# Where an attention kernel loads its queries: during the projection stage, and by SyncE

## The chip, the cores and the metric

One core of one Trainium2 chip. The metric is the device time of one execution in microseconds: the median of several runs. Engines are named as in the profile: PE is TensorE, DVE VectorE, ACT ScalarE, POOL GpSimd, SP SyncE. SPq, ACTq and POOLq are the queues' own instructions, mostly DMA issues.

## What is computed

A transformer block with layer norm after each half, for x of 8 x 1024 x 256: 16 heads of width 16, relative position bias clipped to +-64, and a feed-forward layer whose weights are reduced to a sign times a row mean.

```python
qkv = q @ in_proj_weight.T + in_proj_bias          # 8 x 1024 x 768
qh = qh / sqrt(16)
scores = einsum('bhid,bhjd->bhij', qh, kh)          # 128 maps of 1024 x 1024
rel = clip(pos[None, :] - pos[:, None], -64, 64) + 64
bias = take_along_axis(einsum('bhid,rd->bhir', qh, rel_pe), rel)
attn = softmax(scores + bias); out = (attn @ vh) @ out_w.T + out_b
x = layernorm(x + out)
h = gelu(x @ bw1.T + b1); x = layernorm(x + h @ bw2.T + b2)    # bw = mean|w| * sign(w)
```

## The kernel before

Three stages follow one another, each in a block of its own with a barrier behind it.

**Projection stage** (lines 143 to 569). Eight batches, two buffer halves `a`. For each batch PE turns x (line 487, four banks), ACT copies the banks to `xT` (line 317), PE makes keys, values and queries from it (line 513, line 499, line 513), 12 banks in all. ACT writes the high parts of keys and queries (lines 327 and 336), DVE the low parts and the values (lines 403 and 418). SP stores them to DRAM: `k_scr`, `v_scr`, `q_scr` (lines 263 to 277). ACT waits on `s_store[a]` before it writes keys over those of two batches ago. Ahead of the batches PE turns the projection weights (line 451, jobs 0 to 3), and the table of relative positions is read (`relT`), its differences taken by DVE (lines 389 to 393) and copied by ACT (`rel_parts`, line 303). SP meanwhile writes zeros over the pads of `band_scr`, eight DMAs of 512 KB (line 241). Behind the batches the signs of the feed-forward weights are made and turned (lines 342 and 451), and DVE reduces them to their means (lines 433 and 442).

**Attention stage** (lines 574 to 1170). G = 64 steps, each two heads of one batch; `SLOTS` = 4 buffers for queries, keys and values. Before a step can start, its bands are made, three steps ahead: PE multiplies queries with the table (line 1042), ACT copies the product to `band_out` (line 914; in the profile `carried`), POOL fills its ends (line 829), SP writes it to `band_scr` (line 721), and POOL reads it back skewed, so that each row is shifted by its position (lines 792 to 805). DVE finds row maxima over scores plus band (lines 966 and 977), 24 units ahead, POOL negates them (line 812), PE turns them (line 1060) and SP puts them into two further rows of the queries (line 731), so that the scores come out with the maximum taken off. ACT takes the exponential (line 925), and PE multiplies with the values (line 1109). Each engine's order is written out by hand: steps from -3 to 63, eight pairs of units each (u = 0 to 15).

POOL issues all loads. At its start: the queries of steps 0 and 1, six memsets, the keys of step 0. SP's first work waits for five of the memsets (`s_set`), then writes two rows of ones into the keys (line 754). In the loop:

```python
                def step_of(i, step):
                    if 0 <= step and step + 3 < G:
                        if step > 0:
                            pool.wait_ge(s_sc, cnt(i, 2 * UNITS, step * 2 * UNITS))
                        load_queries(pool, i, step + 3)
                    read_chunk(i, step, 0)
```

`load_queries` issues four DMAs: for each of the two heads one of 128 KB, the high part twice over, and one of 64 KB. `s_sc` counts finished scores: queries of step + 3 go into the buffer that step - 1 read.

**Feed-forward stage** (lines 1172 to 1515): 16 iterations of projection, layer norm, two layers and layer norm.

Of the kernel before, what the change touches and what calls it, by code (L numbers as in the profile page):

```python
# [5 lines left out]
F32 = mybir.dt.float32  # L6
F32R = mybir.dt.float32r
# [24 lines left out]
def post_ln_block(nc, x, w_in, b_in, w_out, b_out, rel, w1, b1, w2, b2, out):  # L32
# [24 lines left out]
    with outer:  # L57
# [52 lines left out]
        x_rows = x.rearrange("b t e -> (b t) e")  # L110

# [27 lines left out]
        with ExitStack() as ctx:  # L139
# [12 lines left out]
            zeros = sb("zeros", [P, NT, P], F32)  # L152
# [5 lines left out]
            w_in_s = sb("w_in_s", [P, 6, E], F32)  # L158
            w_out_s = sb("w_out_s", [P, 2, E], F32)
# [8 lines left out]
            relT = sb("relT", [D, R], F32)  # L168
# [3 lines left out]
            alpha2_wide = sb("alpha2_wide", [P, 2, P], F32)  # L172
            s_win = sem("projection_weights_in")
            s_w = sem("other_weights_in")
# [17 lines left out]
            jobs = []  # L192
# [16 lines left out]
            xT = sb("xT", [P, 2, KE, HALF + T], F32)  # L209
            q_parts = sb("q_parts", [P, 2, PARTS, 2, T], F32R)  # L210
            k_parts = sb("k_parts", [P, 2, PARTS, 2, KCOLS - P], F32R)
            v_s = sb("v_s", [P, 2, NG, NT, HG, VC], F32)

# [17 lines left out]

            block = ctx.enter_context(nc.Block())

            @block.sync
            def _(sp):

                sp.dma_start(w_in_s[:], w_in.rearrange("(j p) e -> p j e", p=P)).then_inc(s_win, 16)
                sp.dma_start(relT[:], rel.rearrange("r d -> d r"), allow_slow_non_contiguous=True).then_inc(s_relT, 16)
                sp.wait_ge(s_set, 3)
                for a in range(SLOTS * HG):  # L240
                    sp.dma_start(flat(band_scr, a * NT * P * BAND_ROW,
                                      [[BAND_ROW, P], [P * BAND_ROW, NT], [1, P]]),
                                 zeros[:]).then_inc(s_zero, 16)
# [10 lines left out]
                with sp.Fori(0, B // 2) as i:  # L254
                    for a in range(2):
# [29 lines left out]
            def _(act):  # L285
# [10 lines left out]
                for n in range(0, 4, 2):  # L296
# [5 lines left out]
                act.wait_ge(s_dve, 3)  # L302
                nc.scalar.activation(rel_parts[:, 0, :], rel_d[:], ACT.Copy).then_inc(s_rel, 1)
                act.dma_start(b1_col[:], b1.rearrange("(j p) -> p j", p=P),
                              allow_slow_non_contiguous=True).then_inc(s_rows, 16)
                act.dma_start(bo_row[:], flat(b_out, 0, [[0, P], [1, E]])).then_inc(s_rows, 16)
                act.dma_start(b2_row[:], flat(b2, 0, [[0, P], [1, E]])).then_inc(s_rows, 16)
                with act.Fori(0, B // 2) as i:
                    for a in range(2):
# [12 lines left out]
                        act.wait_ge(s_store[a], i * 16 * STORES + 16 * STORES)  # L322
                        for m in range(2):
# [16 lines left out]
                act.wait_ge(s_w, 16 * 3)  # L340
# [3 lines left out]
                for n in range(4, len(jobs), 2):  # L344
                    evacuate(n)

            @block.gpsimd
            def _(pool):
# [7 lines left out]
                nc.gpsimd.memset(zeros[:], 0.0).then_inc(s_set, 1)  # L356
# [12 lines left out]
            def _(dve):  # L369
# [10 lines left out]
                for n in range(1, 4, 2):  # L380
# [12 lines left out]
                                        ALU.subtract).then_inc(s_dve, 1)  # L393
                dve.wait_ge(s_rel, 1)
# [52 lines left out]
            def _(pe):  # L447
# [14 lines left out]
                pe.wait_ge(s_eva, 2)  # L462
                pe.wait_ge(s_evd, 2)
                pe.wait_ge(s_dve, 1)
# [54 lines left out]
                pe.wait_ge(s_w, 16 * 3)  # L519
                pe.wait_ge(s_lo, 8 * B + 8)  # L520
                for n in range(4, len(jobs)):
# [13 lines left out]
        with ExitStack() as ctx:  # L535
# [26 lines left out]
            queries = sb("queries", [P, SLOTS, T], F32R)  # L562
# [28 lines left out]
            s_q = [sem(f"queries_in{a}") for a in range(SLOTS)]  # L591
# [11 lines left out]
            s_passed = sem("waits_passed")  # L603
            s_mm = sem("minus_max_split")
# [83 lines left out]
            def load_queries(eng, i, c):  # L688
# [871 lines left out]
```

## Time and profile before

| | us |
|---|---|
| median of 3 runs | 2368.68 |
| lowest, highest | 2364.39, 2369.45 |
| the profiled execution | 2367.33 |
| its span, from first to last instruction | 2365.6 |
| PE busy in it | 2227.5 |
| DVE, ACT, POOL busy | 1740.6, 1573.1, 1085.1 |

The projection stage fills the span up to 222.8 us; the first scores of step 0 come at 281 us. All rows below are of the one profiled execution, and their times are counted from the start of its span. An engine's busy time leaves out DMA issues and waits. In a timeline, rows that repeat are merged: the first number is the start, the second the length of the whole group.

### The profile page before, as it was taken

What the parts mean: (1) busy time and instruction counts of PE and PEld (TensorE: products, weight loads), DVE (VectorE), ACT (ScalarE), POOL (GpSimd) and SP (SyncE); (2) the same over time, 40 slices, a digit from 0 to 9 for tenths busy, and PEclk for the clock granted to TensorE, in tenths of its full rate; (3) what the DMA queues carried; (4) which work ended last, traced back from release to release, by engine and by line L of the source; (5) the groups of instructions that cost most, each with busy time, mean ns of one, the idle gap of its engine ahead of it and who ended that gap; (6) DMA issues with size and microseconds to landing.
All of it is one profiled execution on the core that took longest, in us unless ns stands there. A gap on an engine that the chain in (4) does not pass through costs nothing. (4 is left out here: it accounts for less than half of the span.)

```text
span 2365.6 us, 47819 instructions
## 1 busy us (share of the span) xinstructions
PE 2227.5 (94%) x14580; PEld 1262.2 (53%) x14580; DVE 1740.6 (74%) x3446; ACT 1573.1 (66%) x2193; POOL 1085.1 (46%) x1803
## 2 busy tenths in 40 slices
PE   7996799999999999999999999999999998899997
PEld 4554344544444444444444444444444443688886
DVE  3444677777777777777777777777777772688885
ACT  3443277777777777777777777777777776466776
POOL 1001444455444554455554545545455441567663
PEclk9998599999999999999999999999999999899999
DMA  9987877777777777777777777777777762334321
GB/s 327 363 315 270 220 204 210 212 202 208 211 209 213 199 212 212 207 211 202 209 212 210 211 201 209 216 208 211 200 211 214 209 189 71 101 102 111 111 65 45
DMA packets 334570, 468.55 MB, mean 198 GB/s; under 512 B 89797, under 2 KB 262550, under 8 KB 334486
## 3 DMA queue, kind: packets, MB, share of 16 engines
q0 software_dynamic: 120960, 215.78, 34.4%
q1 hardware_dynamic: 203030, 243.06, 32.3%
q10 hardware_dynamic: 10496, 8.79, 1.2%
q8 instruction: 29, 0.48, 0.1%
q14 instruction: 55, 0.45, 0.1%
HBM read 244.73 MB, written 221.25 MB: 197 GB/s over the span
## 5 line engine op out<-in xcount | busy, mean ns | idle before, releaser
L925 ACT ACTIVATE probs<-weigh_ps 128x1024 f32<-128x1024 f32 x1024 | 1048.9, 1025 | 471.0 <-PE weigh_ps L1092 467.4
L977 DVE CUSTOM_DVE_ANT_1 ring_ps<-ring_ps,band_all 128x512 f32<-128x512 f32 x1008 | 680.9, 715 | 264.3 <-PE ring_ps L1053 263.9
L1053 PE MATMUL ring_ps<-keys,queries 48*128 48x512 f32 x2048 | 827.4, 468 | 34.8 <-DVE partial_max L966 9.5
L1092 PE MATMUL weigh_ps<-queries,keys 50*128 50x512 f32 (+3 forms) x2688 | 751.2, 386 | 1.3 <-ACT probs L925 0.6
L966 DVE TENSOR_REDUCE partial_max<-ring_ps 128x2 f32<-128x1024 f32 x512 | 627.8, 1226 | 114.6 <-PE ring_ps L1053 79.7
L1053 PEld LDWEIGHTS ring_ps<-keys,queries 48*128 48x128 f32 x2048 | 371.1, 187 | 519.0 <-issue 398.0
L1109 PE MATMUL sum_ps<-probs,values 128*32 128x512 f32 x4096 | 546.7, 606 | 0.1
L829 POOL COPY carried<-carried 128x252 f32<-128x252 f32 x430 | 159.2, 395 | 560.8 <-ACT carried L914 560.8
L1077 PE MATMUL weigh_ps<-ident,band_all 128*128 128x128 f32 x2048 | 363.4, 290 | 19.1 <-ACT carried L914 16.3
L1092 PEld LDWEIGHTS weigh_ps<-queries,keys 50*128 50x128 f32 x2688 | 356.8, 186 | 14.8 <-ACT probs L925 9.5
L1077 PEld LDWEIGHTS weigh_ps<-ident,band_all 128*128 128x128 f32 x2048 | 213.8, 141 | 249.5 <-ACT probs L925 104.6
L792 POOL DMA_DIRECT2D band_all<-band_scr x320 | 227.3, 714 | 55.6 <-DMA band_scr<-carried 36.3
L914 ACT ACTIVATE carried<-weigh_ps 128x260 f32<-128x260 f32 (+1 forms) x512 | 209.3, 409 | 2.4 <-PE weigh_ps L1042 2.4
L1042 PE MATMUL weigh_ps<-rel_terms,queries 48*128 48x130 f32 (+1 forms) x1024 | 172.1, 302 | 13.7 <-DMA queries<-q_scr 12.5
L1331 DVE TENSOR_TENSOR hidden<-gelu,hidden 128x512 fp32r<-128x512 f32 x128 | 143.8, 1140 | 46.7 <-ACT hidden L1432 45.5
L1501 PE MATMUL hid_ps<-x1T,sign1T 128*128 128x512 f32 x512 | 144.3, 404 | 12.6 <-ACT hidden L1432 11.3
L1515 PE MATMUL out_ps<-sign2T,hidden 128*128 128x256 f32 x1024 | 150.5, 291 | 0.6 <-ACT hidden L1432 0.6
L1430 ACT ACTIVATE gelu<-hid_ps,b_col,alpha 128x512 f32<-128x512 f32 x128 | 99.7, 779 | 76.7 <-PE hid_ps L1501 54.1
L977 DVE DVE_READ_ACCUMULATOR2_ANT partial_max<- 128x1 f32 x1024 | 145.3, 142 | 0.0
L1515 PEld LDWEIGHTS out_ps<-sign2T,hidden 128*128 128x128 f32 x1024 | 138.1, 189 | 9.4 <-ACT hidden L1432 0.8
L1042 PEld LDWEIGHTS weigh_ps<-rel_terms,queries 48*128 48x128 f32 x1024 | 106.5, 190 | 51.8 <-ACT probs L925 29.3
L513 PE MATMUL bank<-xT,wT 128*128 128x512 f32 x256 | 115.0, 603 | 16.2 <-ACT xT L317 16.2
(121 smaller groups left out, 1854.2 us busy)
## 6 DMA issues: line engine op xcount, KB each, us to landing
band_scr<-carried SPq DMA_DIRECT2D x256, 512.0 KB, 4.8
band_all<-band_scr POOLq DMA_DIRECT2D x128, 512.0 KB, 5.5
band_all<-band_scr POOLq DMA_DIRECT2D x128, 256.0 KB, 4.6
keys<-k_scr POOLq DMA_DIRECT2D x128, 240.0 KB, 8.3
k_scr<-k_parts SPq DMA_DIRECT2D x16, 1792.0 KB, 8.7
q_scr<-q_parts SPq DMA_DIRECT2D x16, 1024.0 KB, 7.5
queries<-q_scr POOLq DMA_DIRECT2D x128, 128.0 KB, 3.8
o_scr<-weighted_s SPq DMA_DIRECT2D x64, 256.0 KB, 7.3
```

Of the source, the lines that this page charges most:

```text
L792: pool.dma_start(band[:, c % SLOTS, m, :, e, c0:c1], flat(band_scr, band_base(c, m) + e * P * BAND_ROW + offset, [[BAND_ROW - 1, P], [2 * ...
L829: last = nc.gpsimd.tensor_copy(out[:, :, e, NARROW:2 * P], flat(end, 0, [end.ap[0], end.ap[1], [0, P - 2]]))
L914: nc.scalar.activation(kept[:, :, 0:width], product[:, :, 0:width], ACT.Copy).then_inc(s_be, 1)
L925: nc.scalar.activation(probs[:, u % PROBS], weigh_ps[weigh_of["scores", at]][:], ACT.Exp).then_inc(s_pr, 1)
L966: nc.vector.reduce_max(partial_max[:, g, :, e, 0], ring_ps[:, first:second + 1], AX_X).then_inc(s_seen, HG)
L977: nc.vector.tensor_tensor_reduce(out=both, in0=both, in1=bias, scale=1.0, scalar=LOWEST, op0=ALU.add, op1=ALU.max, accum_out=partial_max[: ...
L1042: last = nc.tensor.matmul(product, query_rows(c, h, ROWS, tile * P, (tile + 1) * P), moving, start=True, stop=True, tile_position=(h * ROW ...
L1053: nc.tensor.matmul(dst, query_rows(c, h, ROWS, tile * P, (tile + 1) * P), key_rows(c, h, ROWS, c0, c0 + 512), start=True, stop=True, tile_ ...
L1077: nc.tensor.matmul(weigh_ps[weigh_of["scores", at]][:, h, e * P:(e + 1) * P], band[:, c % SLOTS, tile // 2, h, tile % 2, side * P:(side + ...
L1092: last = nc.tensor.matmul(weigh_ps[weigh_of["scores", at]][:, h, e0 * P:e1 * P], key_rows(c, h, QROWS, k0, k0 + P), query_rows(c, h, QROWS ...
L1109: last = nc.tensor.matmul(sum_ps[r0:r0 + 32, :], values[:, c % SLOTS, v0:v0 + 32], probs[:, (2 * n + g) % PROBS, h], start=(n == 0), stop= ...
L1515: last = nc.tensor.matmul(out_ps[:, t], hidden[:, it % 2, c, j, t * P:(t + 1) * P], sign2T[:, j], start=(c == 0 and j == 0), stop=(c == 1 ...
```

## The change

1. `queries` and its semaphores are moved out of the attention stage. SP loads the queries of steps 0 and 1 in the projection stage, right behind batch 7's stores. The room is found by laying other buffers over one another: the weights as read over `xT[:, 1]`, the zeros over `k_parts[:, 1]`, `relT` over `alpha2_wide`, and in the last stage `x1T` over `queries`.
2. The opening: ACT no longer copies the table's differences (DVE does) and no longer issues three loads of biases (SP does, behind `w1` and `w2`). The output weights are read right behind the projection weights and turned by PE before the first batch; PE waits for ACT's copy of them. ACT waits for the zero writes before batch 1's keys.
3. All other query loads go from POOL to SP: step 2's at step -2, u = 13, and those of step + 3 at u = 1, with the same wait on `s_sc`.
4. POOL starts the attention stage with the keys of step 0, then does the memsets.

```diff
@@ projection stage, SP
-                sp.dma_start(relT[:], rel.rearrange("r d -> d r"), allow_slow_non_contiguous=True).then_inc(s_relT, 16)
+                sp.dma_start(w_out_s, w_out.rearrange("(j p) e -> p j e", p=P)).then_inc(s_wout, 16)
+                sp.dma_start(relT, rel.rearrange("r d -> d r"), allow_slow_non_contiguous=True).then_inc(s_relT, 16)
...
-                sp.dma_start(w_out_s[:], w_out.rearrange("(j p) e -> p j e", p=P)).then_inc(s_w, 16)
...
+                sp.dma_start(b1_col[:], b1.rearrange("(j p) -> p j", p=P),
+                             allow_slow_non_contiguous=True).then_inc(s_rows, 16)
+                sp.dma_start(bo_row[:], flat(b_out, 0, [[0, P], [1, E]])).then_inc(s_rows, 16)
+                sp.dma_start(b2_row[:], flat(b2, 0, [[0, P], [1, E]])).then_inc(s_rows, 16)
...
+                sp.wait_ge(s_store[0], 2 * 16 * STORES)
+                load_queries(sp, 0, 0)
+                load_queries(sp, 0, 1)
@@ projection stage, ACT
-                act.wait_ge(s_dve, 3)
-                nc.scalar.activation(rel_parts[:, 0, :], rel_d[:], ACT.Copy).then_inc(s_rel, 1)
-                act.dma_start(b1_col[:], b1.rearrange("(j p) -> p j", p=P),
-                              allow_slow_non_contiguous=True).then_inc(s_rows, 16)
-                act.dma_start(bo_row[:], flat(b_out, 0, [[0, P], [1, E]])).then_inc(s_rows, 16)
-                act.dma_start(b2_row[:], flat(b2, 0, [[0, P], [1, E]])).then_inc(s_rows, 16)
+                evacuate(4)
+                act.wait_ge(s_dve, 2)
...
+                        if a == 1:
+                            act.wait_ge(s_zero, 16 * (SLOTS * HG + 1))
@@ projection stage, DVE
+                dve.wait_ge(s_dve, 3)
+                nc.vector.tensor_copy(rel_parts[:, 0, :], rel_d[:]).then_inc(s_rel, 1)
@@ projection stage, PE
-                pe.wait_ge(s_eva, 2)
+                pe.wait_ge(s_dve, 1)
+                pe.wait_ge(s_wout, 16)
+                turn_weights(4)
+                pe.wait_ge(s_eva, 3)
@@ attention stage, SP's unit(i, step, u)
+                    if step == -2 and u == 13:
+                        load_queries(sp, 0, 2)
+                    if u == 1 and 0 <= step and step + 3 < G:
+                        if step > 0:
+                            sp.wait_ge(s_sc, cnt(i, 2 * UNITS, step * 2 * UNITS))
+                            sp.sem_inc(s_passed_sp, 1)
+                        load_queries(sp, i, step + 3)
@@ attention stage, POOL
-                    if 0 <= step and step + 3 < G:
-                        if step > 0:
-                            pool.wait_ge(s_sc, cnt(i, 2 * UNITS, step * 2 * UNITS))
-                        load_queries(pool, i, step + 3)
...
-                    if step == -2:
-                        load_queries(pool, 0, 2)
...
-                load_queries(pool, 0, 0)
-                load_queries(pool, 0, 1)
+                load_keys(pool, 0, 0)
...
-                load_keys(pool, 0, 0)
@@ feed-forward stage
-            x1T = sb("x1T", [P, 2, 2, KE, TOK], F32R)
+            x1T = queries[:].rearrange("p (a c) (m t) -> p a c m t", c=2, m=KE)
```

## Rows read from the trace of the kernel before

**Rows 1.** Waits, 400 to 1900 us: who for whom, total, times, longest.

```profile
DVE ring_ps L977 <- PE ring_ps L1053: 241.0, 444, 1.1
...
POOL band_all L792 <- DMA band_scr<-carried: 20.5, 24, 2.2
```

**Rows 2.** Timeline, opening: start, length, engine, line, out<-in, [idle before <-releaser].

```profile
5.36 22.55 SPq L241 DMA_DIRECT2D band_scr<-zeros  x8
...
7.41 2.83 PE L451 MATMUL bank<-ident,w_in_s 128*128 128x128 f32 x12 [2.45 <-DMA w_in_s<-attn_in_proj_weight_dram]
...
11.44 1.96 PE L487 MATMUL bank<-ident,x_s 128*128 128x128 f32 x16 [1.21 <-DMA x_s<-in_L_attn_q_dram]
...
15.38 0.52 ACT L303 ACTIVATE rel_parts<-rel_d 16x384 fp32r<-16x384 f32 x1 [4.89 <-DVE rel_d L392]
...
18.08 1.08 ACT L317 ACTIVATE xT<-bank 128x512 f32<-128x512 f32 x2 [2.17 <-issue]
...
20.51 8.84 PE L513 MATMUL bank<-xT,wT 128*128 128x512 f32 x16 [7.11 <-ACT xT L317]
```

**Rows 3.** Waits of the projection stage, 0 to 224 us.

```profile
PE bank L513 <- ACT xT L317: 16.2, 8, 7.1
```

**Rows 4.** Windows: busy of five engines, granted clock, DMA share, GB/s.

```profile
16.00:17.00 1.00, 0.00 (x0) 0.00 (x0) 0.48 (x1) 0.00 (x0) 0.00 (x0) 1.00 1.15 346
...
23.00:24.00 1.00, 1.00 (x2) 0.34 (x1) 0.00 (x0) 0.00 (x0) 0.00 (x0) 0.50 1.35 301
...
296.00:298.00 2.00, 2.00 (x18) 1.49 (x20) 1.30 (x5) 1.24 (x2) 0.00 (x0) 0.74 0.78 221
```

**Rows 5.** Timeline of the projection stage's end.

```profile
203.71 7.03 PE L513 MATMUL bank<-xT,wT 128*128 128x512 f32 x16
...
222.68 0.08 DVE L442 DVE_READ_ACCUMULATOR2_ANT alpha<- 128x1 f32 x1
```

**Rows 6.** SP's own waits, 0 to 224 us.

```profile
SPq L282 <- DMA q_scr<-q_parts: 8.0, 1, 8.0
```

**Rows 7.** Timeline of the boundary and the attention stage's first work.

```profile
223.70 0.64 POOL L692 DMA_DIRECT2D queries<-q_scr  x1 [0.53 <-issue]
...
228.06 0.41 POOL L872 MEMSET band_all<- 128x256 f32 x1
...
229.83 1.48 SPq L754 DMA_DIRECT2D keys<-ones  x2
...
230.91 0.69 PE L1042 MATMUL weigh_ps<-rel_terms,queries 48*128 48x130 f32 x4 [12.54 <-DMA queries<-q_scr]
...
232.67 5.14 SPq L721 DMA_DIRECT2D band_scr<-carried  x4
...
241.59 1.47 POOL L792 DMA_DIRECT2D band_all<-band_scr  x2 [9.49 <-issue]
...
246.50 1.23 DVE L966 TENSOR_REDUCE partial_max<-ring_ps 128x2 f32<-128x1024 f32 x1 [23.74 <-DMA band_all<-band_scr]
```

**Rows 8.** Batch 0's last stores, their landing (last column), batch 2's first key.

```profile
44.90 3.37 SPq L277 DMA_DIRECT2D q_scr<-q_parts  x2
...
q_scr<-q_parts SPq DMA_DIRECT2D x2, 1024.0 KB, 13.8
...
72.13 0.31 ACT L327 ACTIVATE k_parts<-bank,bk_right 128x64 fp32r<-128x64 f32 x1 [2.15 <-PE bank L513]
```

**Rows 9.** DMA issues of the page: count, KB each, us to landing.

```profile
band_scr<-carried SPq DMA_DIRECT2D x256, 512.0 KB, 4.8
...
queries<-q_scr POOLq DMA_DIRECT2D x128, 128.0 KB, 3.8
```

**Rows 10.** GpSimd's timeline in one step of the loop.

```profile
1003.87 0.80 POOL L805 DMA_DIRECT2D band_all<-band_scr  x1 [0.34 <-issue]
...
1015.28 0.65 POOL L692 DMA_DIRECT2D queries<-q_scr  x1
...
1030.76 0.80 POOL L805 DMA_DIRECT2D band_all<-band_scr  x1 [0.34 <-issue]
```

More of the change, by code:

```diff
@@ L110, in post_ln_block, with load_queries @@
         x_rows = x.rearrange("b t e -> (b t) e")
+        queries = sb_in(outer, "queries", [P, SLOTS, T], F32R)
+        s_q = [sem_in(outer, f"queries_in{a}") for a in range(SLOTS)]
+        def load_queries(eng, i, c):
+            for h in range(HG):
+                r0 = h * ROW_TILE
+                part = [q_scr[p, i * SLOTS + c, h * D:(h + 1) * D] for p in range(PARTS)]
+                eng.dma_start(queries[r0:r0 + 2 * D, c % SLOTS].bitcast(F32),
+                              over(part[0], 2, 0)).then_inc(s_q[c % SLOTS], 16)
+                eng.dma_start(queries[r0 + 2 * D:r0 + 3 * D, c % SLOTS].bitcast(F32),
+                              part[1]).then_inc(s_q[c % SLOTS], 16)
         def load_heads(sp, it, raw):
@@ L172, in post_ln_block @@
             alpha2_wide = sb("alpha2_wide", [P, 2, P], F32)
+            relT = alpha2_wide[0:D].rearrange("p j c -> p (j c)")[:, 0:R]
             s_win = sem("projection_weights_in")
[L174 removed]
+            s_w = sem("hidden_weights_in")
+            s_wout = sem("output_weights_in")
             s_bias = sem("projection_biases_in")
@@ L190, in post_ln_block, with key_pieces @@
             s_evd = sem("evacuated_dve")
+            xT = sb("xT", [P, 2, KE, HALF + T], F32)
+            w_in_s = xT[:, 1].rearrange("p m t -> p (m t)")[:, 0:6 * E].rearrange("p (j e) -> p j e", j=6)
+            w_out_s = xT[:, 1].rearrange("p m t -> p (m t)")[:, 6 * E:8 * E].rearrange("p (j e) -> p j e", j=2)
+            q_parts = sb("q_parts", [P, 2, PARTS, 2, T], F32R)
+            k_parts = sb("k_parts", [P, 2, PARTS, 2, KCOLS - P], F32R)
+            v_s = sb("v_s", [P, 2, NG, NT, HG, VC], F32)
+            zeros = k_parts[:, 1, 0, 0, 0:NT * P].bitcast(F32).rearrange("p (n c) -> p n c", n=NT)
+            PRODUCTS = 12
+            token = sb("token", [P, 2], F32)
+            STORES = 2 * PARTS + PARTS + 1
+            s_passed = sem("waits_passed1")
+            s_turned = sem("x_turned")
+            s_job = sem("product_ready")
+            s_xev = sem("xT_ready")
+            s_vev = sem("v_ready")
+            s_hi = sem("high_part_ready")
+            s_lo = sem("low_part_ready")
+            s_store = [sem(f"stored{a}") for a in range(2)]
+            def key_pieces(half):
+                if half == 0:
+                    return [(0, HALF, RIGHT * P, bk_right), (HALF, 512, RIGHT * P, bk_left), (2 * P, 512, -2 * P, bk_right)]
+                return [(0, 512, RIGHT * P + 512, bk_left), (0, 512, 512 - 2 * P, bk_right)]
             jobs = []
@@ L343, in _ @@
                 nc.scalar.activation(sgn2, w2_s, ACT.Sign).then_inc(s_sgn, 1)
-                for n in range(4, len(jobs), 2):
+                for n in range(FIRST_SIGN + 1, len(jobs), 2):
                     evacuate(n)
@@ L518, in _ @@
                                     job += 1
-                pe.wait_ge(s_w, 16 * 3)
+                pe.wait_ge(s_w, 16 * 2)
                 pe.wait_ge(s_lo, 8 * B + 8)
-                for n in range(4, len(jobs)):
+                for n in range(FIRST_SIGN, len(jobs)):
                     if n == FIRST_SIGN:
@@ L590, in post_ln_block @@
             s_one = sem("ones_in")
-            s_q = [sem(f"queries_in{a}") for a in range(SLOTS)]
             s_k = [sem(f"keys_in{a}") for a in range(SLOTS)]
@@ L685, in post_ln_block @@
             block = ctx.enter_context(nc.Block())
-            def load_queries(eng, i, c):
-                for h in range(HG):
-                    r0 = h * ROW_TILE
-                    part = [q_scr[p, i * SLOTS + c, h * D:(h + 1) * D] for p in range(PARTS)]
-                    eng.dma_start(queries[r0:r0 + 2 * D, c % SLOTS].bitcast(F32),
-                                  over(part[0], 2, 0)).then_inc(s_q[c % SLOTS], 16)
-                    eng.dma_start(queries[r0 + 2 * D:r0 + 3 * D, c % SLOTS].bitcast(F32),
-                                  part[1]).then_inc(s_q[c % SLOTS], 16)
             def load_keys(eng, i, c):
```

34 lines of the change are left out of this document (5 added, 29 removed).

## The prediction, made before the changed kernel ran

> **What bounds the kernel now.** I read the waits of the attention loop first, because it fills some 1,600 of the 2,366 us. There VectorE waits only for TensorE, by about 0.5 us a time, and nothing on TensorE's side waits for a DMA; the one wait for a DMA in 1,500 us is GpSimd's for written bands, 20.5 us in 24 places [rows 1]. So the loop goes by TensorE, and a change of who issues a load can't shorten it. It can only lengthen it, if a band arrives late. What can be won lies where TensorE stands still: at the opening, and between the projection stage and the attention stage.
>
> **The opening**, read from the timeline in order of time. TensorE turns batch 0's x from 11.44 to 13.40. ScalarE could empty the first bank some 0.6 us after 11.44, but is still waiting for the table (the copy of rel_d, 15.38), and then issues three DMAs (the 2.17 us of issue ahead of its next copy). Its first xT copy starts at 18.08, and the first product at 20.51 [rows 2]. TensorE waits 7.1 us for xT there and (16.2 - 7.1) / 7 = 1.3 us at each of the other seven batches [rows 3]. The pause has an after-effect: the granted clock is still 1.00 at 16 to 17 us, over 2.5 us into the pause, but 0.50 at 23 to 24 us [rows 4], so the 16 products take 8.84 us [rows 2] against 7.03 us at the full clock [rows 5].
>
> **The boundary.** VectorE ends the projection stage at 222.76 [rows 5]; SP's wait for the last store ends earlier, 8.0 us after its last issue at 213.46, so at 221.5 [rows 6]. GpSimd then issues eight query loads in 4.36 us (223.70 to 228.06), and its memsets only after them. TensorE starts at 230.91, when the first queries are in. SP sends the rows of ones at 229.83 (until 231.31) and the first band write at 232.67, as soon as ScalarE has two bands ready, 1.76 us after TensorE's start. GpSimd sees it landed only at 241.5, 8.8 us later, reads it back, and VectorE begins its maxima at 246.50 [rows 7]. From there VectorE works nearly without a gap until the first scores, so the step that sets the end of the lead-in is the first band, not the first query.
>
> **The change part by part: opening.** (a) The copy of rel_d goes to VectorE and three DMA issues to SP; out of ScalarE's way come 4.9 us of waiting and 2.7 us of copying and issuing (15.38 to 18.08). (b) Added ahead of x: four transposes of w_out, 2.83 / 12 = 0.24 us each at this point [rows 2], so 0.94 us, from 10.24 to 11.2, and a ScalarE copy of a 128x512 bank of about 0.55 us (half of the pair at 18.08 [rows 2]), on which TensorE waits. x's transposes then start at 12.0 with the handovers, 0.5 us later than now. They could start at once if w_out's 256 KB cost the others nothing (11.4); at the worst w_out lands late: w_in, three times as large, is in at 7.4, so a third of those 7.4 us more is 9.9; twice as much is 12.4, with x then at 14.1. (c) From 12.0: 1.96 us of transposes and the usual 1.3 us of waiting for xT, so products from 15.3 in place of 20.51: **5.2 us** (ends 3.1 and 5.8). (d) With a pause of 1.3 us as at the other batches the clock should stay at 1.00, which gives 8.84 - 7.03 = **1.8 us** (ends 0 and 1.8). Opening: 7.0 us.
>
> (e) What covers the moved work. VectorE has nothing to do before the first key piece at some 18.5 us; the table's differences are ready at 15.4 now [rows 2] and a little later behind w_out, and its work on them ends near 18; a delay there has the banks of four later jobs as cover. SP is busy with the zero writes until 27.9 anyway [rows 2]; three more issues put batch 0's stores back by 2 to 3 us. Who waits for those: ScalarE, before it writes batch 2's keys. Now the last store of batch 0 is issued by 48.3 and lands 13.8 us later, at 62, and the keys start at 72.1 [rows 8]; 7 us earlier that is 65.1. The stores are limited by the DMA engines, not by when their data is ready, so they land at 60 to 64. I count nothing, with 3 us of cover left. ScalarE's new wait for the zero writes before batch 1's keys comes at 41, with the zero writes issued by 28.5: nothing. The transposes of w_out leave the end of the stage, where VectorE's chain of reductions ends last: nothing.
>
> **Boundary.** (f) The eight query loads go to SP behind batch 7's last stores, in the shade of VectorE's reductions. SP needs some 4 to 8 us to issue them from 213.5, before 222.8. The first four have to move behind the stores: at best they are in when the stage opens at 223.1, at worst as long after 221.5 as they took from GpSimd (7.2 us [rows 7]), at 228.7. I take 225.4. TensorE starts 5.5 us earlier. (g) GpSimd issues four key loads in place of eight query loads first, half of 4.36 us, so memsets and SP's ones move 2.1 us up, to 227.7. (h) SP's first band write: ones until 229.2, and bands ready at 225.4 + 1.8 = 227.2; so it goes at 229.4, **3.3 us** earlier, and the bound has moved from ScalarE's copies to GpSimd's memsets and SP. (i) It takes 8.8 us to land now, against a median of 4.8 us [rows 9]. These are its bounds. In front of it now lie the ones, and beside it GpSimd's keys and the rest of the queries; afterwards the keys are mostly gone, but the ones and step 1's queries are ahead in the same queue. I take 7.3 us, nearer to the write's own row: **1.5 us**. Reading back costs 5.0 us as now. VectorE starts at 241.7 in place of 246.50: **4.8 us** (ends 3.3 and 7.3; 0 if the queries in SP's queue hold the ones back). The keys of step 0 are issued 6.2 us earlier and needed 4.8 us earlier.
>
> **Loop.** (j) GpSimd loses four issues of some 0.6 us a step, which nothing waited for. (k) SP gains them, and a wait at u = 1 for the end of the last step's scores. Behind that wait stands the band write of u = 3, whose bands TensorE makes only after those scores: it can't be held up. Nothing. Queries are wanted half a step after they are issued: nothing. (l) x1T in the queries' place is written behind the stage's barrier: nothing.
>
> **Sum:** 5.2 + 1.8 + 4.8 = 11.8 us, from 2367.3 us in the profiled run (span 2365.6) to 2355.5. The median is 1.35 us above the profiled run, so 2356.9. The clock at step 0 is a loose end: it is at 0.50 from the boundary until about 297 us [rows 4]; I assume that this stretch moves with the rest. If it rises one pair of key tiles earlier or later, that is 1.5 us either way.
>
> **Rivals.** (1) One half is given back, by one of two ways: batch 0's stores land after 65.1 and hold ScalarE at batch 2 (3 to 7 us lost of the opening), or the query loads hold the ones and the first band write until 232.7 (the boundary gives 0). For it: the DMA engines are full in the opening (shares of 1.15 and 1.35 [rows 4]). Against it: the slack worked out above. 2361 to 2364, say 2362. (2) Nothing of it shows: the opening's gain is lost in the DMA backlog and the boundary's in the same queue. 2364 to 2373. Against it: two separate places would have to fail. (3) **Slower.** In the loop the query loads now stand in SP's queue with the band writes. A 128 KB load lands in 3.8 us [rows 9]; two of them a step, one after the other on the same engines, are 7.6 us in which bands written or read on those engines are late. A band read issued at 1003.87 lands by about 1009.4 and is used when the next step opens, at 1015.3 at the latest; the step is 1030.76 - 1003.87 = 26.9 us [rows 10]. So the slack there is 5 to 6 us, and 8 or more for reads issued at the step's start, when the queries move. It decides from 11.8 / 60 = 0.2 us a step; with 0.5 us a step it would be 30 us more, 2387 us. Against it: the wait of GpSimd for bands is now 2.2 us at most [rows 1].
>
> Beside this: the Trainium skill (DMA: Bandwidth & Descriptors, Why a DMA increments its semaphore by 16 and not by 1) says that a DMA whose slowest dimensions share only the divisor 2 runs on two engines; from SP always the lowest-numbered two, from GpSimd a pair that moves round. The doubled half of each query load has such a shape, and so have the ones, and by that rule rival 3's series is real where before it was spread out. That the one write behind the ones took 8.8 us agrees with it; no row here names an engine.
>
> **How the numbers follow.** Forecast 0.56, rival 1 0.23, rival 2 0.14, rival 3 0.07. A measurement of this kernel can tell 0.2%, 4.7 us, from no change. Faster by more: forecast and rival 1, 0.79; within: 0.14; slower: 0.07. The range takes the forecast's own ends (gains of 5 to 16), rival 1 whole and part of rival 2: 2352 to 2365.5.
>
> **What would show it.** First xT copy near 12.7 and first product near 15.3, with the clock at 1.00 at 16 to 20 us; ScalarE's keys of batch 2 waiting for TensorE and not for a store; VectorE's end of the stage at 215.8; TensorE's first band product 2 to 3 us after it in place of 8.2; SP's first band write 6.6 us after it in place of 9.9; VectorE's first maximum 19 us after it in place of 23.7; the step at 26.9 us as before. The forecast is wrong if batch 2 waits for stores, if the first band write takes over 9 us to land, or if the step lengthens by 0.1 us.

## The result

The changed kernel takes 2547.8 us (median of 4 runs, 2540.2 to 2555.6) against 2368.9 us before. The ratio is 1.076, with an interval of 1.073 to 1.078: 179 us slower, where 11.8 us faster were forecast. The loss lies in the attention loop. These lines are from the page of the changed kernel; the last one shows 87.6 us in which TensorE's band products wait for queries, which cost 12.5 us in all before, at the boundary alone:

```profile
span 2553.8 us, 47841 instructions
PE 2328.6 (91%) x14580; PEld 1295.8 (51%) x14580; DVE 1744.6 (68%) x3447; ACT 1580.6 (62%) x2192; POOL 939.9 (37%) x1547
...
PEclk9996789989999899999999988889998999899999
...
L1052 PE MATMUL weigh_ps<-rel_terms,queries 48*128 48x130 f32 (+1 forms) x1024 | 170.3, 309 | 97.3 <-DMA queries<-q_scr 87.6
```

From 320 us to the end of the loop the granted clock's digits (a tenth of full speed each, 64 us a digit) are 8 and 9, where they were all 9 before. The waits between 400 and 1900 us (who waited for whom: total us, times, longest) have a line for queries on TensorE's side that was not there before, and GpSimd's waits for written bands are up to 7.5 us long in place of 2.2 [rows 1]:

```profile
DVE ring_ps L987 <- PE ring_ps L1063: 352.6, 398, 6.4
...
POOL band_all L823 <- DMA band_scr<-carried: 225.5, 75, 7.5
...
PE weigh_ps L1052 <- DMA queries<-q_scr: 66.9, 43, 4.0
```

How the loss divides is read from one window of 1,500 us, 400 to 1900, of each kernel. The columns are busy us and instructions of PE, PEld, DVE, ACT and POOL, granted clock, DMA share and GB/s. First the kernel before, then the changed one:

```profile
400.00:1900.00 1500.00, 1466.21 (x10420) 739.32 (x10420) 1181.53 (x2341) 1084.34 (x1450) 744.56 (x1447) 1.00 0.74 209
```

```profile
400.00:1900.00 1500.00, 1396.43 (x9320) 688.14 (x9314) 1057.37 (x2094) 976.38 (x1297) 553.39 (x1098) 0.93 0.64 186
```

A step was 26.9 us [rows 10], so 10,420 matmuls were 55.8 steps, 186.9 each. 9,320 are 49.9 steps: a step now takes 30.1 us, 3.2 us more. TensorE's busy time a step goes from 26.3 to 28.0 us (+1.7) for the same matmuls, and its idle time from 0.6 to 2.1 us (+1.5), of which the waits for queries are 1.3 (66.9 us in 49.9 steps). So about half of the loss is waiting, and the other half is the same work at a lower clock. 61 steps by 3.2 us are 195 us; the span grew by 188.

One step in the loop shows the wait itself. SP issues the four loads of the queries behind a band write, at 1005.60 to 1008.35:

```profile
1004.88 0.36 SPq L732 DMA_DIRECT2D band_scr<-carried  x1
1005.60 0.72 SPq L118 DMA_DIRECT2D queries<-q_scr  x1
1006.51 0.43 SPq L120 DMA_DIRECT2D queries<-q_scr  x1
1007.13 0.68 SPq L118 DMA_DIRECT2D queries<-q_scr  x1
1008.00 0.35 SPq L120 DMA_DIRECT2D queries<-q_scr  x1
```

TensorE's first product of them starts at 1020.49, 14.9 us after the first issue, and a little later a matmul takes 0.79 us where 0.49 us is usual:

```profile
1018.68 0.49 PE L1063 MATMUL ring_ps<-keys,queries 48*128 48x512 f32 x1
...
1020.49 0.33 PE L1052 MATMUL weigh_ps<-rel_terms,queries 48*128 48x130 f32 x2 [1.32 <-DMA queries<-q_scr]
...
1024.39 0.79 PE L1063 MATMUL ring_ps<-keys,queries 48*128 48x512 f32 x1
```

From GpSimd a load of 128 KB landed in 3.8 us from its issue (median) [rows 9].

The granted clock around this pause (windows of the same view as above) is at its upper level, 2.4 GHz, just behind the pause, then at half of it, 1.2 GHz, for 6 us in which TensorE is busy throughout, and then up again:

```profile
1021.00:1022.00 1.00, 1.00 (x10) 0.20 (x2) 0.00 (x0) 0.32 (x1) 0.28 (x2) 1.00 0.39 152
1023.00:1029.00 6.00, 6.00 (x27) 2.72 (x26) 3.14 (x6) 2.71 (x5) 2.69 (x5) 0.50 0.41 124
1030.00:1031.00 1.00, 1.00 (x12) 0.20 (x10) 0.66 (x1) 0.77 (x1) 0.00 (x0) 1.00 0.99 262
```

So the one pause of 1.32 us is followed by a stretch at half clock that is several times as long.

**Opening and boundary.** Up to the end of the projection stage the change works much as meant. These lines answer to [rows 2] and [rows 5]:

```profile
12.04 3.52 PE L508 MATMUL bank<-ident,x_s 128*128 128x128 f32 x16 [2.17 <-DMA x_s<-in_L_attn_q_dram]
13.19 0.60 ACT L332 ACTIVATE xT<-bank 128x512 f32<-128x512 f32 x1 [2.69 <-PE bank L508]
...
16.45 7.13 PE L534 MATMUL bank<-xT,wT 128*128 128x512 f32 x16 [0.89 <-ACT xT L332]
...
216.89 0.08 DVE L461 DVE_READ_ACCUMULATOR2_ANT alpha<- 128x1 f32 x1
```

The stage ends at 216.97 in place of 222.76, 5.8 us sooner. At the boundary, which answers to [rows 7], 3.2 us of it are given back:

```profile
221.66 0.69 PE L1052 MATMUL weigh_ps<-rel_terms,queries 48*128 48x130 f32 x4 [9.08 <-DMA queries<-q_scr]
...
221.89 5.26 SPq L772 DMA_DIRECT2D keys<-ones  x2
...
227.20 20.59 SPq L732 DMA_DIRECT2D band_scr<-carried  x5
...
238.94 1.47 POOL L810 DMA_DIRECT2D band_all<-band_scr  x2 [16.93 <-DMA band_scr<-carried]
...
243.87 1.23 DVE L976 TENSOR_REDUCE partial_max<-ring_ps 128x2 f32<-128x1024 f32 x1 [26.89 <-DMA band_all<-band_scr]
```

TensorE does start sooner after the stage's end (4.7 us in place of 8.2), but it still waits for the queries, though SP had issued those loads from 207.97 on. SP's two issues of the ones take 5.26 us in place of 1.48, and the first band write is read back 11.7 us after its issue began. VectorE begins 26.9 us after the stage's end in place of 23.7.

The DMA share (the mean busy share of the core's 16 DMA engines, second number from the end) shows what the query loads ran on. Between 217 and 218 us the stores of the stage are in and GpSimd's first load is issued only at 217.79, so what moves is SP's query loads. In the kernel before, GpSimd's eight query loads were on their way at 227 to 228 us. First the changed kernel, then the one before, then the changed kernel while SP issues the first band write (that single issue lasts from 227.20 to 233.32):

```profile
217.00:218.00 1.00, 0.00 (x0) 0.00 (x0) 0.00 (x0) 0.00 (x0) 0.34 (x3) 0.50 0.12 49
```

```profile
227.00:228.00 1.00, 0.00 (x0) 0.00 (x0) 0.00 (x0) 0.00 (x0) 1.00 (x3) 0.50 0.65 103
```

```profile
228.00:233.00 5.00, 0.07 (x2) 0.07 (x2) 0.00 (x0) 0.00 (x0) 0.00 (x0) 0.50 0.13 46
227.20 6.12 SPq L732 DMA_DIRECT2D band_scr<-carried  x1
```

A share of 0.12 of 16 engines is the work of two (0.12 x 16 = 1.9; an estimate, since no row names an engine). It is 0.13 while the band write is being issued, with the ones ahead of it and the last keys not yet in, and 1.05 from 234 us on.

### The profile page after: what moved, and what is told of

Read it like the earlier page. It is cut to its first block and busy times, and to the rows that moved or that the text cites. A ratio compares the mean times of both kernels' runs of the same rounds, so it can differ in the third digit from the quotient of the medians.

```text
span 2553.8 us, 47841 instructions
## 1 busy us (share of the span) xinstructions
PE 2328.6 (91%) x14580; PEld 1295.8 (51%) x14580; DVE 1744.6 (68%) x3447; ACT 1580.6 (62%) x2192; POOL 939.9 (37%) x1547
## 5 line engine op out<-in xcount | busy, mean ns | idle before, releaser
L1063 PE MATMUL ring_ps<-keys,queries 48*128 48x512 f32 x2048 | 856.7, 487 | 43.4 <-DVE partial_max L976 14.6
L1102 PE MATMUL weigh_ps<-queries,keys 50*128 50x512 f32 (+3 forms) x2688 | 792.5, 402 | 1.4 <-ACT probs L935 0.9
L1063 PEld LDWEIGHTS ring_ps<-keys,queries 48*128 48x128 f32 x2048 | 384.8, 197 | 548.6 <-issue 398.1
L1119 PE MATMUL sum_ps<-probs,values 128*32 128x512 f32 x4096 | 586.3, 646 | 0.1
L1087 PE MATMUL weigh_ps<-ident,band_all 128*128 128x128 f32 x2048 | 385.2, 303 | 19.5 <-ACT carried L924 16.6
L1102 PEld LDWEIGHTS weigh_ps<-queries,keys 50*128 50x128 f32 x2688 | 374.1, 194 | 14.9 <-ACT probs L935 9.5
L1087 PEld LDWEIGHTS weigh_ps<-ident,band_all 128*128 128x128 f32 x2048 | 232.6, 149 | 275.9 <-issue 170.1
L1052 PE MATMUL weigh_ps<-rel_terms,queries 48*128 48x130 f32 (+1 forms) x1024 | 170.3, 309 | 97.3 <-DMA queries<-q_scr 87.6
L810 POOL DMA_DIRECT2D band_all<-band_scr x320 | 227.5, 715 | 37.9 <-DMA band_scr<-carried 37.3
L823 POOL DMA_DIRECT2D band_all<-band_scr x128 | 100.5, 785 | 332.0 <-DMA band_scr<-carried 273.4
L1511 PE MATMUL hid_ps<-queries,sign1T 128*128 128x512 f32 x512 | 144.1, 404 | 16.1 <-ACT hidden L1442 13.2
```

What stands on the lines that cost most here:

```text
L810: pool.dma_start(band[:, c % SLOTS, m, :, e, c0:c1], flat(band_scr, band_base(c, m) + e * P * BAND_ROW + offset, [[BAND_ROW - 1, P], [2 * ...
L1052: last = nc.tensor.matmul(product, query_rows(c, h, ROWS, tile * P, (tile + 1) * P), moving, start=True, stop=True, tile_position=(h * ROW ...
L1063: nc.tensor.matmul(dst, query_rows(c, h, ROWS, tile * P, (tile + 1) * P), key_rows(c, h, ROWS, c0, c0 + 512), start=True, stop=True, tile_ ...
L1087: nc.tensor.matmul(weigh_ps[weigh_of["scores", at]][:, h, e * P:(e + 1) * P], band[:, c % SLOTS, tile // 2, h, tile % 2, side * P:(side + ...
L1102: last = nc.tensor.matmul(weigh_ps[weigh_of["scores", at]][:, h, e0 * P:e1 * P], key_rows(c, h, QROWS, k0, k0 + P), query_rows(c, h, QROWS ...
L1119: last = nc.tensor.matmul(sum_ps[r0:r0 + 32, :], values[:, c % SLOTS, v0:v0 + 32], probs[:, (2 * n + g) % PROBS, h], start=(n == 0), stop= ...
```

## The experiments

**Theory A.** A query load that reads 16 rows of DRAM twice into 32 rows of SBUF has an outer dimension of 2 on its source side (below, a doubled load). From SP's queue such loads run on few DMA engines, the same ones for each, so the two of a step stand in line; the ones begin with a dimension of 2 as well. The queries land late, TensorE pauses for them, and its clock falls. The Trainium skill (DMA: Bandwidth & Descriptors, Why a DMA increments its semaphore by 16 and not by 1) says of such shapes that they run on two engines, from SP always on the lowest-numbered two and from GpSimd on a pair that moves round. The share of 0.12 with SP's doubled loads on their way, against 0.65 with GpSimd's, agrees with it. **Rival B:** the loss comes from elsewhere in the change. **Rival C:** any query load in SP's queue, at that place and time, comes late. **Rival D:** SP's issues themselves take too long. **Rival E:** 128 KB or 32 rows in one DMA are too much for SP's queue, whatever the source's shape.

**Loop loads back to GpSimd.** The changed kernel, with the loads of steps 2 to 63 taken from SP's list and put where they stood before in GpSimd's:

```diff
-                    if step == -2 and u == 13:
-                        load_queries(sp, 0, 2)
-                    if u == 1 and 0 <= step and step + 3 < G:
...
-                        load_queries(sp, i, step + 3)
...
+                        load_queries(pool, i, step + 3)
...
+                        load_queries(pool, 0, 2)
```

> The changed kernel with all query loads but those of steps 0 and 1 back on GpSimd, as before the change; those two stay with SP in the projection stage. Theory A (in the loop, SP's query loads land late because the doubled halves run one after another on few DMA engines, TensorE waits for them and its clock falls): the loop's step is 26.9 us again, TensorE waits for no query in it, and the time is the one before less what the first maximum of VectorE gains in the changed kernel (243.87 against 246.50): 2364 to 2368 us. Rival B (the loss comes from another part of the change: buffers laid over one another, or the reordered stage ahead): still over 2500 us.

Measured: 2366.1 us, ratio 0.9996 (0.9986 to 1.0006), so within measurement the time before; no wait for queries in the loop, and the clock there is 1.00. VectorE's first maximum comes at 243.58, as in the changed kernel. Rival B falls.

**Opening alone.** Steps 0 and 1 go back to GpSimd too, ahead of the keys, so that only the work around x's transposes is left of the change.

```diff
-                sp.wait_ge(s_store[0], 2 * 16 * STORES)
-                load_queries(sp, 0, 0)
-                load_queries(sp, 0, 1)
...
-                load_keys(pool, 0, 0)
+                load_queries(pool, 0, 0)
+                load_queries(pool, 0, 1)
...
+                load_keys(pool, 0, 0)
```

> As the run before it, and the queries of steps 0 and 1 too are loaded by GpSimd in the attention stage, ahead of the keys: what is left of the change is the opening. The projection stage should end at 217.0 us as in the changed kernel (before: 222.8), and VectorE's first maximum come 23.7 us after it as before the change, so at 240.7: 5.8 us gained, 2362 to 2364 us. If theory A is right in this part too, this is 2 to 4 us faster than the run before it, because SP's loads of steps 0 and 1 hold the ones and the first band write back. Rival: loading them early still helps, and this run is the slower of the two.

Measured: 2364.1 us, ratio 0.9986 (0.9976 to 0.9996): the opening alone is worth 0.14%, some 3 to 4 us. In its trace VectorE's first maximum comes 5.1 us sooner than before the change, so a part of that gain does not reach the end; where it goes was not followed. The maximum comes at 241.41, 2.2 us sooner than in the run before (23.8 us after the stage's end in place of 26.8), and the median is 2.0 us less. The trace thus says that SP's early loads of steps 0 and 1, in this shape, do harm; a difference of 2 us between two kernels' medians is hardly clear of noise here.

**The loop's loads alone.** The kernel before, with only the loads of steps 2 to 63 moved to SP, behind the first band write of a step (`u == 1`) and the same wait for `s_sc`.

```diff
-                        load_queries(pool, i, step + 3)
+                        load_queries(sp, i, step + 3)
```

> The kernel before with one part of the change alone: the query loads of steps 2 to 63 go from GpSimd to SP. Theory A: the whole loss, TensorE waits for queries by 1 to 2 us a step, mean clock near 0.93, 2540 to 2565 us. Rival B: 2369 us.

Measured: 2567.3 us (one run), 2 us above what was expected; mean clock 0.929. The waits, 400 to 1900 us, have the two lines of the changed kernel again:

```profile
POOL band_all L815 <- DMA band_scr<-carried: 223.4, 74, 6.9
...
PE weigh_ps L1050 <- DMA queries<-q_scr: 73.8, 43, 3.9
```

TensorE waits 1.5 us a step for queries (73.8 us in 49.5 steps). One part of the change, four DMAs a step from another queue and at their place in it, makes the whole loss.

**Sixteen rows.** The changed kernel, in which the doubled load is cut in two:

```diff
-                eng.dma_start(queries[r0:r0 + 2 * D, c % SLOTS].bitcast(F32),
-                              over(part[0], 2, 0)).then_inc(s_q[c % SLOTS], 16)
+                for n in range(2):
+                    eng.dma_start(queries[r0 + n * D:r0 + (n + 1) * D, c % SLOTS].bitcast(F32),
+                                  part[0]).then_inc(s_q[c % SLOTS], 16)
```

> The changed kernel, in which each doubled half (32 rows, the same 16 of DRAM twice) is loaded by two DMAs of 16 rows; who issues, when, and where in SP's queue stays the same, with six issues in place of four. Theory A (few engines): the loads spread over all engines and land within 5 to 6 us, TensorE waits for no query in the loop, the step is 26.9 us, and the boundary gains too: 2355 to 2362 us. Rival C (what costs is the place in SP's queue, behind a band write and ahead of the next, or the time of issue): still over 2500 us. Rival D (SP's issues themselves take too long): slower than the changed kernel.

Measured: 2361.1 us, ratio 0.9971 (0.9961 to 0.9980). The step is back, at the full clock:

```profile
400.00:1900.00 1500.00, 1465.92 (x10407) 736.47 (x10407) 1179.63 (x2339) 1083.16 (x1447) 619.04 (x1224) 1.00 0.74 208
```

The same bytes come from the same queue, issued at the same place, in more DMAs; rivals C and D fall. The same 16 rows of DRAM are still read twice, so reading them twice is not by itself what costs. At the boundary TensorE starts 0.3 us after the projection stage's end, at 218.67, and waits for no load:

```profile
218.67 0.69 PE L1053 MATMUL weigh_ps<-rel_terms,queries 48*128 48x130 f32 x4 [4.70 <-PEq L151]
...
223.27 1.48 SPq L773 DMA_DIRECT2D keys<-ones  x2
224.80 18.74 SPq L733 DMA_DIRECT2D band_scr<-carried  x5
...
234.70 1.47 POOL L811 DMA_DIRECT2D band_all<-band_scr  x2 [11.31 <-DMA band_scr<-carried]
```

Of the changed kernel's two lines on waits for DMAs one remains, GpSimd's wait for written bands, 145.6 us in 54 places in the loop and 2.8 us at the longest: GpSimd has four issues less a step and waits where it had work before. No engine waits for a DMA of GpSimd's in the loop. So of the 225.5 us of this wait in the changed kernel only a part can be lateness of bands.

**Thirty-two rows of source.** The changed kernel; each doubled load reads 32 rows that follow one another in DRAM. The second sixteen are another head's, so this kernel computes other scores.

```diff
-                              over(part[0], 2, 0)).then_inc(s_q[c % SLOTS], 16)
+                              q_scr[0, i * SLOTS + c, 0:2 * D]).then_inc(s_q[c % SLOTS], 16)
```

> The changed kernel, all query loads by SP, with one thing different: the source of each 128 KB load is 32 rows of DRAM one behind the other in place of the same 16 rows twice. The number of DMAs, their bytes, their rows in SBUF, their place and time of issue are the same; the data of the second 16 rows is that of another head, so the scores aren't the reference's. Theory A (the source's outer dimension of 2 is what keeps the load on few engines): no wait for queries, 2358 to 2364 us. Rival E (32 rows of SBUF or 128 KB in one DMA from SP are slow in themselves): as the changed kernel, over 2500 us.

Measured: 2359.7 us (one run), and the loop has no wait for queries:

```profile
400.00:1900.00 1500.00, 1465.32 (x10402) 736.09 (x10400) 1179.30 (x2337) 1082.77 (x1445) 617.14 (x1224) 1.00 0.74 208
```

For these loads the page has a time from issue to landing (last column), which it lacks for the doubled ones from SP:

```profile
queries<-q_scr SPq DMA_DIRECT2D x128, 128.0 KB, 5.0
```

So 128 KB can land from SP in 5.0 us in this loop, behind the same band write. The number of DMAs, bytes and SBUF rows are those of the changed kernel. Only the source's shape differs, 32 rows in place of 2 by 16, and with it 188 us. Rival E falls; this is the cleanest of the runs. Whether 2 by 16 different rows would cost the same as the same 16 twice was not tried.

**The loads divided.** SP issues the two 64 KB loads of a step (`part[1]`, the argument `(1,)`), GpSimd the two doubled ones (`part[0]`, `(0,)`), each with a semaphore of its own:

```diff
-                        load_queries(sp, i, step + 3)
+                        load_queries(sp, i, step + 3, (1,))
...
+                        load_queries(pool, i, step + 3, (0,), True)
```

> The changed kernel, with the loop's query loads divided: SP issues the two 64 KB loads of 16 rows a step, GpSimd the two doubled loads of 128 KB. Theory A (doubled loads in SP's queue run on few engines, one after another): no wait for queries in the loop, step 26.9 us, 2362 to 2368 us. Rival C (any query load in SP's queue comes late): TensorE waits for queries, over 2450 us.

Measured: 2368.5 us (one run), clock 0.977, no wait of TensorE for queries: at the upper edge of what was expected, 0.5 us past it. And the other way round:

```diff
-                        load_queries(sp, i, step + 3)
+                        load_queries(sp, i, step + 3, (0,))
...
+                        load_queries(pool, i, step + 3, (1,), True)
```

> The same division the other way round: SP issues the two doubled loads of 128 KB a step, GpSimd the two of 64 KB. Theory A: the whole loss is here, 2520 to 2560 us, TensorE waits for queries by over 1 us a step. Rival C: between the two, about 2450 us.

Measured: 2501.1 us (one run), clock 0.946, TensorE's band product waits 49.0 us in 42 places:

```profile
PE weigh_ps L1066 <- DMA queries<-q_scr: 49.0, 42, 3.1
```

The loss is with the doubled loads, as theory A has it, but it ends 19 us below the range: with the 64 KB loads in the same queue too, the time is 47 us more, of the 187 us that lie between the changed kernel and the sixteen-row one. Alone in SP's queue they cost nothing (the run before). That they add to a lateness which is already there is my reading; their landing is not in the trace.

**One doubled load a step.** Head 0's is cut in two, head 1's left whole.

```diff
+                if h == 0:
+                    for n in range(2):
+                        eng.dma_start(queries[r0 + n * D:r0 + (n + 1) * D, c % SLOTS].bitcast(F32),
+                                      part[0]).then_inc(s_q[c % SLOTS], 16)
+                else:
```

> The changed kernel with one of the two doubled loads a step cut into two of 16 rows, the other whole; all by SP. Theory A says that the two doubled loads stand in line for the same engines; with one of them the queries land at least 2.5 us and up to 6 us sooner. TensorE's wait was 1.3 us a step in the changed kernel, so it should be gone or nearly: 2360 to 2400 us. If a single doubled load in SP's queue is already too slow (a place in the queue, not a line of two): over 2450 us.

Measured: 2361.2 us (one run), clock 0.980, no wait for queries: as fast as with both cut. So a single doubled load a step in SP's queue is in time; with two of them a step the queries come too late. Up to that point lateness costs nothing.

**Lateness by itself.** The kernel before, all loads by GpSimd, the queries issued behind keys and values:

```diff
-                        load_queries(pool, i, step + 3)
                     read_chunk(i, step, 0)
...
                         load_values(pool, i, step + 3)
+                        load_queries(pool, i, step + 3)
```

> The kernel before, all by GpSimd, but the queries of a step are issued behind its keys and values in place of ahead of them, 9.6 us later by the trace of before (1024.9 in place of 1015.3); they should land near 1031, and TensorE wants them at 1027.9. It tells what lateness alone costs, with the loads on the engines of before. If lateness and the clock that falls in TensorE's pauses are the whole loss of the changed kernel: TensorE waits some 3 us a step, its mean clock falls below 0.95, and the time is 2530 to 2640 us. If busy engines and late bands carry the loss: lateness alone costs little, below 2450 us.

Measured: 3002.2 us (one run), far beyond the range. Its window and its waits:

```profile
400.00:1900.00 1500.00, 1186.02 (x7473) 572.69 (x7470) 847.10 (x1677) 782.17 (x1040) 532.89 (x1038) 0.83 0.53 150
```

```profile
PE weigh_ps L1039 <- DMA queries<-q_scr: 292.3, 40, 8.6
```

TensorE waits 7.3 us a step and not 3: the queries, issued from 1003.72, are used at 1014.39, 10.7 us later, where I had counted 6 us. They now stand behind the keys and values in GpSimd's queue; that this is why was not tested. By the same count as above (7,473 / 186.9 = 40.0 steps) a step is 37.5 us: 10.6 us more, 7.2 of them idle and 3.4 in slower matmuls. So lateness of the queries and the clock are enough for a loss larger than the changed kernel's, without SP's queue. The part of the clock is a third here and a half in the changed kernel: in all 3.2 us a step for 1.5 us more of idle time, and 10.6 us for 7.2.

**The ones.** The sixteen-row kernel, and the ones written row by row, both sides in 16 pieces:

```diff
-                    row = keys[h * ROW_TILE + ROWS:h * ROW_TILE + QROWS].bitcast(F32)
-                    sp.dma_start(flat(row, 0, [row.ap[0], [P, SLOTS * KCOLS // P], [1, P]]),
-                                 flat(ones[:], 0, [ones[:].ap[0], [0, SLOTS * KCOLS // P], [1, P]])
+                    for r in range(2):
+                        at = h * ROW_TILE + ROWS + r
+                        row = keys[at:at + 1].bitcast(F32)
+                        sp.dma_start(flat(row, 0, [row.ap[0], [SLOTS * KCOLS // 16, 16], [1, SLOTS * KCOLS // 16]]),
+                                     ones[:, 0:SLOTS * KCOLS // 16].rearrange("r (a p) -> r a p", a=1)
```

> The sixteen-row kernel of before, and the rows of ones at the start of the attention stage are written by four DMAs whose two sides both begin with 16 pieces of 480 elements, in place of two DMAs of 2 rows by 60 pieces of 128. In the sixteen-row run the first band write is issued at 224.80 and read back only from 234.70, 9.9 us later. Theory A (the ones hold that write back on the few engines that they run on): it lands in 5 to 6 us, VectorE's first maximum comes 4 us sooner than at 239.62, and the time is 2355 to 2359 us against 2361. Rival: the first write's landing is due to the keys and its own size; no change, 2361 us.

Measured: 2357.9 us (4 runs), ratio 0.9957 (0.9941 to 0.9974), the lowest median of this study; its interval overlaps that of the sixteen-row kernel. The trace is clearer: the first band write is read back after 5.4 us in place of 9.9, and its own issue takes SP 0.58 us in place of 4.33. VectorE's first maximum comes 19.0 us after the stage's end in place of 21.3:

```profile
221.59 2.47 SPq L775 DMA_DIRECT2D keys<-ones  x4
...
224.10 15.48 SPq L733 DMA_DIRECT2D band_scr<-carried  x5
...
229.52 1.47 POOL L813 DMA_DIRECT2D band_all<-band_scr  x2 [7.81 <-DMA band_scr<-carried]
```

The issues of the first band write, first of the sixteen-row kernel, then of this one:

```profile
224.80 4.33 SPq L733 DMA_DIRECT2D band_scr<-carried  x1
```

```profile
224.10 0.58 SPq L733 DMA_DIRECT2D band_scr<-carried  x1
```

The same edit in the kernel before, and in the one with the opening alone:

> The kernel before with that one edit, the spread ones, alone. Theory A: the first band write lands 3 us sooner than in 8.8 us, 2364 to 2366 us. Rival: 2368.5 us.

> The opening-alone kernel (all queries by GpSimd, 2364.1 us) with the spread ones: 2360 to 2362 us by theory A, 2364 us by the rival. Against the run of SP's sixteen-row loads with spread ones it shows what early loading is worth once no load stands in line.

Measured: 2368.2 us (1.0002, 0.9992 to 1.0012) and 2366.7 us (0.9989, 0.9979 to 0.9999): nothing gained in either, so theory A's expectation missed both times, and the second is even 2.6 us slower than the opening alone. In the first of them the band write of 232.17 is still read back only at 242.41, 10.2 us later. So in the kernel before it is not the ones that hold that write back. SP issues it there 1.36 us after the last of the ones, and its issue is short already:

```profile
232.67 0.61 SPq L721 DMA_DIRECT2D band_scr<-carried  x1
```

What makes its landing long there is open; the keys and step 1's queries move at the same time, and neither was tried. What the second run does show is the worth of loading the first queries early from SP: with spread ones and sixteen-row loads 2357.9 us, with spread ones and all queries from GpSimd 2366.7 us (the two differ in who loads in the loop as well).

## Why the prediction was wrong

**The loop, step (k): wrong, and it decides.** I wrote that queries are wanted half a step after they are issued, and counted nothing. The only duration of such a load in the prediction is 3.8 us, GpSimd's row [rows 9], given under rival 3. A row of one queue was taken for the other. From SP the queries were there 14.9 us after the first issue, and half a step is 13.4 us. SP's queue is not slow by itself: with 32 rows of source the 128 KB landed in 5.0 us. It is the queue and the doubled shape together. The term should have been 3.2 us a step: 1.5 us of idle time, of which 1.3 us waiting for queries, and 1.7 us for the clock.

**Rival 3 had the place and not the victim or the size.** Two loads a step one after the other on the same engines is what the runs fit: one doubled load is in time, two are not, a source of 32 rows makes both harmless, and at the boundary SP's doubled loads together kept only two engines' worth of the 16 busy. But I asked only who reads bands. GpSimd's waits for bands grew, and TensorE never waited for a band; the queries themselves were late. For a chain of DMAs on few engines I took 7.6 us from the 3.8 us of the other queue, and left out the band write ahead of them and GpSimd's loads on the same engines. 2387 us was the price for 0.5 us a step; it was 3.2. Its chance of 0.07 came from slack that belonged to another transfer. The rule of the Trainium skill that stood beside it was the one to cost: by it the loads of a step stand in line from SP and not from GpSimd. The runs bear this out as far as they can show it: which engines these are is in no trace here.

**The clock: half seen.** I had it for pauses of 7 us at the opening and not for short ones in the loop. Waits for queries of 1.3 us a step were enough for a mean clock of 0.93 in the loop, against 1.00 before; behind the pause shown above the clock was at 0.50 for 6 us.

**Opening, (a) to (d): right in kind, 5.8 us in place of 7.0.** x's transposes start at 12.04 (forecast 12.0). The term that was off is the 1.96 us for them: they take 3.52 us, nearly twice the time each at the same granted clock of 1.00 (why is open), so the products start at 16.45 and not at 15.3, 4.1 us gained in place of 5.2. The clock's term held: 7.13 us for the 16 products against 8.84, 1.7 us of 1.8. ScalarE's keys of batch 2 waited for no store, and the end of the stage followed.

**Boundary, (f) to (i): wrong, by the same mistake.** TensorE started 4.7 us after the stage's end, not 2 to 3. GpSimd's memsets were earlier as said, but the ones took SP 5.26 us to issue and not 1.48, so the first band write came 10.2 us after the stage's end (forecast 6.6, before 9.9), and it took 11.7 us and not 7.3, with 6.12 us for the issue alone. VectorE started 26.9 us after it and not 19. I had named this as the end where the boundary gives 0, and it gave less. With the doubled loads cut it is 21.3 us (239.62 from 218.36), and with the ones spread too 19.0 us.

**The sum** was thus right for another kernel: sixteen-row loads and spread ones give 2357.9 us, where 2356.9 was forecast for the change as written. Even there the 19 us up to the first maximum are in part luck: the first band write went later than forecast (7.4 us after the stage's end for 6.6) and took less (5.4 us for 7.3), and reading it back took more (6.1 us for 5.0).

## What to carry to other kernels

A DMA's time belongs to its queue and its shape together, so a time measured from one queue is no price for the other. Before a load moves from GpSimd to SP, look at the outer dimensions of both its sides, and if one of them is 2 (a row set read twice, two rows of many pieces), cut it or lay it out so that both begin with 16 or 32, as in the three forms that were harmless here. A DMA share near 0.12 while such loads are all that moves is the sign in a trace. Count lateness from the last of such loads in line against the moment the data is wanted, and know that below that moment it is free and above it a TensorE-bound loop pays for the pause and again in clock.

## What the runs showed of the hardware

- 128 KB from the same queue into the same 32 rows of SBUF: from 32 rows of DRAM it costs the loop nothing, from 16 rows read twice 188 us in 61 steps.
- While SP's query loads, four of them doubled, were all that moved, the mean busy share of the 16 DMA engines was 0.12, at 49 GB/s; with GpSimd's eight query loads on their way it was 0.65, at 103 GB/s.
- TensorE's clock in the loop: 1.00 with no wait for queries, 0.95 with 1.0 us of them a step (49.0 us in 51.5 steps), 0.93 with 1.3 us, 0.83 with 7.3 us. One pause of 1.32 us was followed by 6 us at 0.50.
- Issuing can be what is slow: the ones took SP 1.48 us to issue with no query load of SP's ahead of them, and 5.26 us behind eight query loads, four of them doubled; behind sixteen-row loads it was 1.48 us again. The issue of the band write behind the ones took 6.12 us, 4.33 us with sixteen-row loads ahead, and 0.58 us when the ones were spread as well.
- Cutting a load costs little: the first two steps' queries as twelve loads of 64 KB in place of eight cost SP four issues more, and TensorE started 0.3 us after the stage's end in place of 4.7.
